# A four-way row scan and a dynamic-convolution block on one core: reciprocal deviations carried to the channels through DRAM, the norm on GpSimd

## Chip, core and metric

The kernel runs on one core of one Trainium2 chip. The metric is the device time of one launch in microseconds. Three runs of the kernel before gave 893.47 (median), 891.79 and 895.72.

## What is computed

```python
# x: (8, 64, 64, 64) float32
# 1. four scans over rows or columns, each new = cur + relu(conv9(prev)), 64 -> 64 channels
# 2. on the result x, per image (weights 5x5 per image and channel, from the pooled image):
out = depthwise_conv5x5(x, dyn_w(mean(x)))
u = out.mean(1, keepdims=True); s2 = square(out - u).mean(1, keepdims=True)
out = (out - u) * rsqrt(s2 + 1e-6)                 # over the 64 channels
out = ln2_w * out + ln2_b
out = gelu(einsum('bchw,oc->bohw', out, w_expand)) # 64 -> 256, exact gelu
gx = sqrt(sum(square(out), (2, 3)))                # per image and wide channel
nx = gx / (gx.mean(1) + 1e-6)
out = gamma * (out * nx) + beta + out
return einsum('bohw,co->bchw', out, w_shrink) + x  # 256 -> 64
```

## The kernel before

The first part, `scans` (lines 97 to 533), runs the four scans. The change leaves its loops as they are. It ends near 500 us of the profile.

The second part, `block_two` (from line 536), works on 16 units, `UNITS`: a unit is half an image, 32 lines of 64 columns, held as 128 partitions (64 channels times the parity of the line) by 1024 elements (`UCOLS`). The five engines run five programs that are written out by hand and meet at semaphores. Each program walks the same slots `s` from -1 to 20 (`SLOTS_RUN`), and in slot `s` handles several units at different stages. VectorE is in slot `s` when it adds the taps of unit `s`.

The stages of a unit `u`, with the engine and the slot:

- TensorE, slot u-1: `convolve`, five of the 5x5 taps in a split of high and low parts: 30 matmuls of 512 columns in six pieces, into PSUM banks 0 to 3 (two sets, by `u % 2`). They need `x_hi` (ScalarE, `split_high`), `x_lo` (GpSimd, `split_low`) and the diagonal weights (GpSimd, `make_dyn`, once in two units).
- ScalarE, slot u-1: five taps as products (`product`, line 764): one into `part`, four into `prod`. GpSimd adds the four in slot u (`add_product`, line 709).
- VectorE, slot u: ten taps (`take_tap`, line 883), each reading one image and the PSUM sum; the last writes `inner`. Then GpSimd adds `part` to `inner` (`add_inner`, line 722).
- Slot u+1, the statistics over channels: ScalarE squares `inner` (`square`, 772), TensorE sums both with small matmuls (`statistics`, 1075), ScalarE squares the mean (777), VectorE makes the variance (`make_var`, 891 and 893), ScalarE its root (783, after a table load), VectorE the reciprocal `rstd` of 128 x 128 (900). `rstd` holds the reciprocals on 16 of the partitions, by group of columns and line parity.
- Slot u+2: TensorE carries `rstd` to all 128 partitions with a 0/1 matrix, `spread` (`widen`, 1086, four matmuls for each half of the unit), into PSUM bank 7. VectorE multiplies `inner` by it (`norm`, 907, two halves of 512). TensorE expands (`expand`, 1100) into the one pair of banks 4 and 5, four times per unit: for each half `c` of the columns, for each half `m` of the wide channels. ScalarE takes each with `gelu` (795, with a table load per slot) and, at the end of the slot, sums the squares of both `m` (`add_squares`, 807), which wait for all four gelus. The squares are written over the same `squares` buffer that `square` uses.
- After every second unit: `sum_energy`, `root_energy`, `respond` scale the shrinking weights of the image.
- Slot u+5: TensorE `shrink` (1121, two calls), VectorE `finish` (937), SyncE `store` (684).

SyncE's queue holds, per slot, `cross(s + 2)` (lines 675 and 677: two transfers within SBUF that bring the lines of the other parity for the cross taps of unit s+2, once the taps of unit s are done), then `store(s - 5)` (two transfers to DRAM).

## Time and profile before

| what | value |
|---|---|
| median of three runs | 893.47 us |
| the profiled execution's own time | 893.85 us |
| its span, first to last instruction | 892.0 us |
| TensorE busy | 816.9 us (92%) |
| VectorE busy | 604.4 us (68%) |
| ScalarE busy | 433.2 us (49%) |
| GpSimd busy | 454.5 us (51%) |
| granted TensorE clock, mean | 0.971 |

The shares are over the whole span, of which the scans take more than half. Busy time is the time in which an engine has an instruction under way. Idle time in a table stands with the engine's next instruction and the one that released it. A duration in a row runs to the end of the instruction; the next one on the same engine may begin about 0.1 us before that end.

### The profile page before, as it was taken

Reading aid. Unit: us, or ns where it says so; the run is one execution under the profiler, and the core shown is the slowest. Engines: PE = TensorE matmul, PEld = TensorE weight load, DVE = VectorE, ACT = ScalarE, POOL = GpSimd, SP = SyncE. Lnnn points to the kernel's source line nnn. Section 1 sums busy time; section 2 is a strip of 40 time slices with the busy share of each in tenths; the row PEclk is TensorE's granted clock in tenths of the full one; section 3 lists DMA queues with packets and bytes.
Section 4 is the critical chain, followed back from the end, with each engine's and each line's share of the span. In section 5 each row is a group of like instructions: output and inputs, shape, how many; then the busy total and the mean of one; then the engine's idle time right before and its main releaser. Section 6 shows DMA issues by size and latency. Waiting matters only on the chain. (4 is left out here: it accounts for less than half of the span.)

```text
span 892.0 us, 16129 instructions
## 1 busy us (share of the span) xinstructions
PE 816.9 (92%) x5639; PEld 666.5 (75%) x5639; DVE 604.4 (68%) x1127; ACT 433.2 (49%) x520; POOL 454.5 (51%) x443
## 2 busy tenths in 40 slices
PE   5999999999999999999999675889999999999775
PEld 5999999999999999999999654455454555545231
DVE  4666666666666666678888657777887778888722
ACT  5690005777750000000000154798989898988662
POOL 2333333333323333368888466767777776765500
PEclk9999999999999999999999788889999999999997
DMA  6750000000000000000000100110222222223123
GB/s 139 170 141 0 0 0 1 0 0 0 0 1 1 0 0 0 1 1 0 0 0 0 47 0 24 34 36 24 48 47 47 47 47 47 47 47 71 24 48 71
DMA packets 51189, 26.99 MB, mean 30 GB/s; under 512 B 40720, under 2 KB 49104, under 8 KB 51152
## 3 DMA queue, kind: packets, MB, share of 16 engines
q1 hardware_dynamic: 51152, 26.51, 13.2%
q8 instruction: 22, 0.36, 0.2%
q14 instruction: 15, 0.12, 0.0%
HBM read 9.98 MB, written 8.39 MB: 21 GB/s over the span
## 5 line engine op out<-in xcount | busy, mean ns | idle before, releaser
L487 PE MATMUL psum<-line_hi,taps_hi 128*128 128x256 f32 x1270 | 203.0, 292 | 11.8 <-DVE taps_lo L383 8.6
L501 PE MATMUL psum<-line_lo,taps_hi 128*128 128x256 f32 x1270 | 202.5, 291 | 0.8 <-DVE line_lo L436 0.8
L495 PE MATMUL psum<-line_hi,taps_lo 128*128 128x256 f32 x1270 | 202.0, 291 | 0.0
L436 DVE SCALAR_TENSOR_TENSOR line_lo<-psum,rest 128x256 fp32r<-128x256 f32 x254 | 108.2, 426 | 123.6 <-POOL rest L263 115.3
L487 PEld LDWEIGHTS psum<-line_hi,taps_hi 128*128 128x128 f32 x1270 | 177.1, 192 | 13.0 <-issue 9.3
L501 PEld LDWEIGHTS psum<-line_lo,taps_hi 128*128 128x128 f32 x1270 | 176.4, 191 | 2.0 <-DVE line_lo L436 1.8
L495 PEld LDWEIGHTS psum<-line_hi,taps_lo 128*128 128x128 f32 x1270 | 176.7, 191 | 0.0
L263 POOL TENSOR_TENSOR rest<-x,line_hi 128x256 f32<-128x256 f32 x127 | 82.9, 653 | 168.5 <-DVE line_hi L427 168.5
L709 POOL TENSOR_TENSOR part<-part,prod 128x960 f32<-128x960 f32 (+2 forms) x64 | 145.2, 2269 | 24.3 <-ACT part L764 17.5
L315 ACT ACTIVATE by_h<-x (+1 forms) x128 | 85.7, 670 | 106.1 <-DVE x L416 104.5
L263 POOL TENSOR_TENSOR rest<-by_h,line_hi 128x256 f32<-128x256 f32 x127 | 91.5, 721 | 83.4 <-DVE line_hi L427 83.4
L416 DVE TENSOR_TENSOR x<-line_hi,line_lo 128x256 f32 (+1 forms) x190 | 105.5, 555 | 0.2
L883 DVE SCALAR_TENSOR_TENSOR psum<-x,tap_all,psum 128x930 f32<-128x930 f32 (+2 forms) x80 | 96.7, 1209 | 1.3
L1100 PE MATMUL psum<-normed,expand_w 64*128 64x512 f32 x256 | 75.0, 663 | 22.6 <-ACT wide L795 17.1
L764 ACT ACTIVATE prod<-x,tap_all 128x960 f32<-128x960 f32 (+2 forms) x64 | 70.1, 1101 | 37.5 <-POOL part L709 30.1
L883 DVE SCALAR_TENSOR_TENSOR psum<-crossed,tap_cross,psum 128x992 f32<-128x992 f32 (+1 forms) x64 | 80.7, 1261 | 10.3 <-PE psum L1060 9.4
L722 POOL TENSOR_TENSOR inner<-inner,part 128x1024 f32<-128x1024 f32 x16 | 37.9, 2367 | 86.5 <-DVE inner L883 86.5
L795 ACT ACTIVATE wide<-psum,expand_bias 128x1024 f32<-128x1024 f32 x64 | 70.9, 1109 | 20.9 <-PE psum L1100 20.7
L1060 PE MATMUL psum<-x_hi,dyn_hi 128*128 128x512 f32 x160 | 70.3, 439 | 9.1 <-DVE inner L883 5.8
L751 ACT ACTIVATE x_hi<-x 128x1024 fp32r<-128x1024 f32 x16 | 16.7, 1051 | 126.2 <-PEq L106 121.7
L1121 PE MATMUL psum<-wide,shrink_now 128*64 128x512 f32 x256 | 67.1, 653 | 3.7 <-DVE shrink_now L928 2.9
L427 DVE SCALAR_TENSOR_TENSOR line_hi<-psum,x 128x256 fp32r<-128x256 f32 x127 | 54.0, 425 | 21.9 <-PE psum L487 8.6
(129 smaller groups left out, 899.3 us busy)
## 6 DMA issues: line engine op xcount, KB each, us to landing
stage<-in_x_dram SPq DMA_DIRECT2D x32, 256.0 KB, 4.1
out_dram<-x SPq DMA_DIRECT2D x32, 256.0 KB, 4.4
crossed<-x SPq DMA_DIRECT2D x16, 256.0 KB, 3.5
crossed<-x SPq DMA_DIRECT2D x16, 240.0 KB, 3.6
fc_in<-in_L_conv_w_fc_dram SPq DMA_DIRECT2D x2, 100.0 KB
taps<-in_L_conv_k_td_dram SPq DMA_DIRECT2D x2, 80.0 KB, 3.3
taps<-in_L_conv_k_dt_dram SPq DMA_DIRECT2D x2, 80.0 KB, 3.3
taps<-in_L_conv_k_lr_dram SPq DMA_DIRECT2D x2, 80.0 KB, 3.5
```

Of the source, the lines that this page charges most:

```text
L263: pool.tensor_tensor(rest[:, slot % 2, :].rearrange("p (b i) -> p b i", b=B), x_line, line_hi[:, (slot + 1) % SLOTS, :, REACH:REACH + WP]. ...
L315: act.activation(dst, src, ACT.Copy).then_inc(turned, 1)
L416: dve.tensor_tensor(kept_line(s, row_of(s, k)), line_hi[:, made, :, part].bitcast(F32), line_lo[:, made, :, part].bitcast(F32), ALU.add).t ...
L436: dve.scalar_tensor_tensor(out=line_lo[:, (slot + 1) % SLOTS, :, part], in0=as_lines(line_ps[slot][:, 0:LINE]), scalar=0.0, in1=as_lines(r ...
L487: mm = pe.matmul(line_ps[slot][:, 0:LINE], taps_hi[:, s, d, :], line_hi[:, slot, :, d:d + WP], start=(d == 0), stop=(d == OFFSETS - 1))
L495: pe.matmul(line_ps[slot][:, 0:LINE], taps_lo[:, s, d, :], line_hi[:, slot, :, d:d + WP], start=False, stop=False, skip_group_check=True)
L501: mm = pe.matmul(line_ps[slot][:, 0:LINE], taps_hi[:, s, d, :], line_lo[:, slot, :, d:d + WP], start=False, stop=(d == OFFSETS - 1), skip_ ...
L709: pool.tensor_tensor(dst, dst, other, ALU.add).then_inc(part_step, 1)
L795: act.activation(wide[:, m, :, u % WIDE, c * COLS:(c + 1) * COLS], exp_ps[:, :, :], ACT.Gelu, bias=expand_bias[:, m:m + 1]).then_inc(gelu_ ...
L883: dve.scalar_tensor_tensor(out=dst, in0=src, scalar=weight, in1=here, op0=ALU.mult, op1=ALU.add).then_inc(tap_step, 1)
L1060: mm = pe.matmul(conv_ps[:, 2 * (u % 2) + c, :], weight[:, b % 2, n, :, :].rearrange("p o c -> p (o c)"), image[:, u % 2, CROWS * c:CROWS ...
L1100: mm = pe.matmul(exp_ps[:, hp, :], expand_w[half, m, :], normed[half, c, :], start=True, stop=True)
```

## The change

- `rstd` no longer goes through TensorE. SyncE stores it to a DRAM scratch of 2 x 128 x 128 (`spread_rstd`), waits until it has landed, and reads it back with two transfers, one for each line parity, each to 64 partitions (`rstd_wide`, 128 x 1024). `widen`, `spread` and its preparation in the scans go.
- `norm` moves from VectorE (two halves) to GpSimd (one multiplication of 128 x 1024), into a double buffer `normed` for whole units. In GpSimd's program it stands behind `add_inner` of the unit after it, ahead of the products.
- One tap, ("up", 3), moves from ScalarE with its addition on GpSimd to VectorE: eleven taps there, four products, three additions.
- `expand` goes by channels first: both column halves for `m` = 0, then for `m` = 1. So `add_squares` of `m` = 0 stands between the gelus and that of `m` = 1 opens the next slot; both write to a buffer of their own, `dump`. For the last two units, three pairs of PSUM banks serve in turn.
- The statistics, `make_var`, `root` and `rstd` come earlier in the slot; `inner` has two buffers in place of three; the energy of an image is summed one slot later; SyncE issues the store before the cross lines.

The diff, cut to its core:

```diff
 DVE_TAPS = [("cross", 0), ("cross", 1), ("cross", 3), ("cross", 4), ("up", 0), ("up", 4), ("down", 0), ("down", 4),
-            ("down", 3), ("cross", 2)]
+            ("down", 3), ("up", 3), ("cross", 2)]
 MIDDLE = [("down", 2), ("up", 2)]
-SIDES = [("up", 1), ("down", 1), ("up", 3)]
+SIDES = [("up", 1), ("down", 1)]
...
-        INNERS = 3
+        INNERS = 2
+        EXP_SETS = 3
+        FREE_CONV = 4 * (UNITS - 2)
...
-        normed = sb("normed", [P, 2, COLS])
+        rstd_wide = sb("rstd_wide", [P, UCOLS])
+        normed = sb("normed", [P, 2, UCOLS])
+        dump = sb("dump", [P, 2 * UCOLS], BF16)
...
+        rstd_dram = nc.dram_tensor("rstd_dram", [2, P, STAT_COLS], F32, kind="Internal").ap()
...
+        def exp_set(e):
+
+            first = 4 if e < FREE_CONV else (4, 0, 2)[(e - FREE_CONV) % EXP_SETS]
+            return psum[:, first:first + 2, :]
...
+            def spread_rstd(u):
+
+                sp.wait_ge(rstd_ready, u + 1)
+                if u > 1:
+                    sp.wait_ge(rstd_spread, 32 * (u - 1))
+                sp.dma_start(rstd_dram[u % 2], rstd[:, u % 2, :]).then_inc(rstd_stored[u % 2], 16)
+                sp.wait_ge(rstd_stored[u % 2], 16 * (u // 2 + 1))
+                if u > 0:
+                    sp.wait_ge(normed_ready, u)
+                rows = rstd_dram[u % 2].rearrange("(g q) n -> g (q n)", g=4)
+                for h in range(2):
+                    mine = rows[:, SUBS * h * STAT_COLS:SUBS * (h + 1) * STAT_COLS].rearrange("(a g) n -> a g n", a=1)
+                    sp.dma_start(rstd_wide[C * h:C * h + C, :].rearrange("p (g n) -> p g n", g=4),
+                                 mine.to_broadcast([C, 4, SUBS * STAT_COLS])).then_inc(rstd_spread, 16)
+
             cross(0)
             for s in SLOTS_RUN:
+                if s - 1 in range(UNITS):
+                    spread_rstd(s - 1)
+                if s >= 5:
+                    store(s - 5)
                 if s + 2 < UNITS:
                     cross(s + 2)
-                if s >= 5:
-                    store(s - 5)
             sp.wait_ge(stored, 32 * UNITS)
...
+            def norm(u):
+                pool.wait_ge(rstd_spread, 32 * (u + 1))
+                if u > 1:
+                    pool.wait_ge(exp_done, 4 * (u - 1))
+                image = inner[:, u % INNERS, :, :].rearrange("p j w -> p (j w)")
+                pool.tensor_tensor(normed[:, u % 2, :], image, rstd_wide[:, :], ALU.mult).then_inc(normed_ready, 1)
+
             pool.wait_ge(taps_known, 1)
             pool.wait_ge(dyn_ready, 1)
-            for u in range(UNITS):
-                for n in range(1, N_ACT):
-                    add_product(u, n)
-                if u + 2 < UNITS:
-                    split_low(u + 2)
-                if u % 2 == 0 and u // 2 + 1 < B:
-                    make_dyn(u // 2 + 1)
-                add_inner(u)
+            for s in range(UNITS + 2):
+                w, e = s - 1, s - 2
+                if w in range(UNITS):
+                    add_inner(w)
+                if e >= 0:
+                    norm(e)
+                if s < UNITS:
+                    for n in range(1, N_ACT):
+                        add_product(s, n)
+                if s + 2 < UNITS:
+                    split_low(s + 2)
+                if s % 2 == 0 and s // 2 + 1 < B:
+                    make_dyn(s // 2 + 1)
...
-            def gelu(u, c, m):
-                act.wait_ge(exp_done, 2 * (2 * u + c) + m + 1)
+            def gelu(u, m, c):
+                act.wait_ge(exp_done, 4 * u + 2 * m + c + 1)
                 if m == 0 and u >= WIDE:
                     act.wait_ge(out_done, 2 * (u - WIDE) + c + 1)
-                act.activation(wide[:, m, :, u % WIDE, c * COLS:(c + 1) * COLS], exp_ps[:, :, :],
+                act.activation(wide[:, m, :, u % WIDE, c * COLS:(c + 1) * COLS], exp_set(4 * u + 2 * m + c),
                                ACT.Gelu, bias=expand_bias[:, m:m + 1]).then_inc(gelu_done, 1)
 
             def add_squares(u, m):
                 b, h = u // 2, u % 2
-                act.wait_ge(gelu_done, 4 * (u + 1))
+                act.wait_ge(gelu_done, 4 * u + 2 * (m + 1))
                 if h == 0 and b > 0:
                     act.wait_ge(energy_summed, b)
                 if u + m > 0:
                     act.wait_ge(energy_ready, 2 * u + m)
-                if m == 0 and u + 1 < UNITS:
-                    act.wait_ge(stats_done, u + 2)
-                act.activation(squares[:, :].bitcast(BF16).rearrange("p (a n) -> p a n", a=2),
+                act.activation(dump[:, :].rearrange("p (a n) -> p a n", a=2),
                                wide[:, m, :, u % WIDE, :], ACT.Square,
                                accum_out=energy[:, m, h:h + 1]).then_inc(energy_ready, 1)
...
-                w, e, v = s - 1, s - 2, s - 5
-
-                def products(lo, hi):
-                    if s + 1 < UNITS:
-                        for n in range(lo, min(hi, N_ACT)):
-                            product(s + 1, (n + 1) % N_ACT)
-
+                w, e, n = s - 1, s - 2, s - 3
+                if n in range(UNITS):
+                    add_squares(n, 1)
                 if 2 <= s + 2 < UNITS:
                     split_high(s + 2)
-                for i in range(4):
-                    if e in range(UNITS):
-                        gelu(e, i // 2, i % 2)
-                    products(i, i + 1)
-                    if i == 1 and w in range(UNITS):
-                        square(w)
-                products(4, N_ACT)
+                if w in range(UNITS):
+                    square(w)
+                if s + 1 < UNITS:
+                    product(s + 1, 0)
                 if w in range(UNITS):
                     square_mean(w)
                     root(w)
-                if 0 < e <= UNITS and e % 2 == 0:
-                    root_energy(e // 2 - 1)
-                if e in range(UNITS):
-                    add_squares(e, 0)
-                    add_squares(e, 1)
+                if n in range(UNITS) and n % 2 == 1:
+                    root_energy(n // 2)
+                for i, between in enumerate(((1, 2), (), (3,), ())):
+                    if e in range(UNITS):
+                        gelu(e, i // 2, i % 2)
+                    if i == 1 and e in range(UNITS):
+                        add_squares(e, 0)
+                    for p in between:
+                        if s + 1 < UNITS:
+                            product(s + 1, p)
...
-                    dve.wait_ge(normed_ready, 2 * (u - INNERS + 1))
+                    dve.wait_ge(normed_ready, u - INNERS + 1)
...
-                if e in range(UNITS):
-                    norm(e, 0)
-                take(1)
+                take(2)
                 if v >= 0:
                     finish(v, 0)
                 take(2)
-                if e in range(UNITS):
-                    norm(e, 1)
-                take(2)
-                if v >= 0:
-                    finish(v, 1)
-                if 0 < e <= UNITS and e % 2 == 0:
-                    sum_energy(e // 2 - 1)
-                take(2)
+                if n in range(UNITS) and n % 2 == 1:
+                    sum_energy(n // 2)
                 if w in range(UNITS):
                     make_var(w)
                 take(1)
                 if w in range(UNITS):
                     make_rstd(w)
                 take(1)
-                if 0 < e <= UNITS and e % 2 == 0:
-                    respond(e // 2 - 1)
+                if v >= 0:
+                    finish(v, 1)
+                take(1)
+                if n in range(UNITS) and n % 2 == 1:
+                    respond(n // 2)
                 take(N_DVE)
...
+            def expand(u, m, c):
+                e = 4 * u + 2 * m + c
+                if e == 0:
+                    pe.wait_ge(weights_ready, 1)
+                if c == 0 and m == 0:
+                    pe.wait_ge(normed_ready, u + 1)
+                if e == FREE_CONV + 1:
+                    pe.wait_ge(tap_step, N_DVE * UNITS)
+                if 0 < e <= FREE_CONV:
                     pe.wait_ge(gelu_done, e)
-                else:
-                    pe.wait_ge(weights_ready, 1)
+                elif e >= FREE_CONV + EXP_SETS:
+                    pe.wait_ge(gelu_done, e - EXP_SETS + 1)
                 for hp in range(2):
                     half = slice(C * hp, C * hp + C)
-                    mm = pe.matmul(exp_ps[:, hp, :], expand_w[half, m, :], normed[half, c, :], start=True, stop=True)
+                    mm = pe.matmul(exp_set(e)[:, hp, :], expand_w[half, m, :], normed[half, u % 2, c * COLS:(c + 1) * COLS],
+                                   start=True, stop=True)
                 mm.then_inc(exp_done, 1)
...
-                at_e(widen, 0)
-                at_v(shrink, 0)
-                at_e(expand, 0, 0)
+                        shrink(v, c)
+
+                at_v(0)
                 conv(0)
-                at_e(widen, 1)
-                at_e(expand, 0, 1)
-                at_v(shrink, 1)
-                at_e(expand, 1, 0)
                 conv(1)
-                at_e(expand, 1, 1)
+                if w in range(UNITS):
+                    statistics(w)
+                at_e(0, 0)
+                at_v(1)
                 conv(2)
-                at_w(statistics)
+                at_e(0, 1)
                 conv(3)
+                if n in range(UNITS) and n % 2 == 1:
+                    respond(n // 2)
+                at_e(1, 0)
                 conv(4)
-                if 0 < e <= UNITS and e % 2 == 0:
-                    respond(e // 2 - 1)
                 conv(5)
+                at_e(1, 1)
```

GpSimd's program in block_two, in the middle of the steady run: one slot with and one without the diagonal weights. `inner<-inner,part` is `add_inner`, `part<-part,prod` is `add_product`, `x_lo` is `split_low`. Before:

```order
L722 TENSOR_TENSOR inner<-inner,part 128x1024
L709 TENSOR_TENSOR part<-part,prod 128x960
L709 TENSOR_TENSOR part<-part,prod 128x15x63
L709 TENSOR_TENSOR part<-part,prod 128x16x63
L709 TENSOR_TENSOR part<-part,prod 128x15x63
L704 TENSOR_TENSOR x_lo<-x,x_hi 128x16x64
L731 TENSOR_TENSOR dyn_hi<-ident_half,tap_hi 128x640
L731 TENSOR_TENSOR dyn_lo<-ident_half,tap_lo 128x640
```

and with the change:

```order
L744 TENSOR_TENSOR inner<-inner,part 128x1024
L762 TENSOR_TENSOR normed<-inner,rstd_wide 128x1024
L731 TENSOR_TENSOR part<-part,prod 128x960
L731 TENSOR_TENSOR part<-part,prod 128x15x63
L731 TENSOR_TENSOR part<-part,prod 128x16x63
L726 TENSOR_TENSOR x_lo<-x,x_hi 128x16x64
L753 TENSOR_TENSOR dyn_hi<-ident_half,tap_hi 128x640
L753 TENSOR_TENSOR dyn_lo<-ident_half,tap_lo 128x640
```

The multiplication stands where the fourth addition's time was, and ahead of the other three.

ScalarE's program from one table load for gelu on (`wide` is a gelu, `prod` and `part` a product, `squares<-inner` is `square`, `mean_sq` the square of the mean). Before:

```order
L795 ACT_TABLE_LOAD
L795 ACTIVATE wide<-psum,expand_bias 128x2x512
L764 ACTIVATE prod<-x,tap_all 128x960
L795 ACTIVATE wide<-psum,expand_bias 128x2x512
L764 ACTIVATE prod<-x,tap_all 128x15x63
L772 ACTIVATE squares<-inner 128x1024
L795 ACTIVATE wide<-psum,expand_bias 128x2x512
L764 ACTIVATE prod<-x,tap_all 128x16x63
L795 ACTIVATE wide<-psum,expand_bias 128x2x512
L764 ACTIVATE prod<-x,tap_all 128x15x63
L764 ACTIVATE part<-x,tap_all 128x1024
L777 ACTIVATE mean_sq<-psum 128x128
```

and with the change, from the start of a slot's statistics:

```order
L785 ACTIVATE x_hi<-x 128x16x64
L804 ACTIVATE squares<-inner 128x1024
L798 ACTIVATE part<-x,tap_all 128x1024
L809 ACTIVATE mean_sq<-psum 128x128
L815 ACT_TABLE_LOAD
L815 ACTIVATE std<-var,eps_col 128x128
L827 ACT_TABLE_LOAD
L827 ACTIVATE wide<-psum,expand_bias 128x2x512
L798 ACTIVATE prod<-x,tap_all 128x960
L798 ACTIVATE prod<-x,tap_all 128x15x63
L827 ACTIVATE wide<-psum,expand_bias 128x2x512
L837 ACTIVATE dump,energy<-wide 128x2048
```

Square, mean and root stood behind the gelus and products, and now stand ahead of them; a sum of squares stands among the gelus.

## Rows read from the trace of the kernel before

**Rows 1.** The page: the span, and busy time by engine.
```profile
span 892.0 us, 16129 instructions
PE 816.9 (92%) x5639; PEld 666.5 (75%) x5639; DVE 604.4 (68%) x1127; ACT 433.2 (49%) x520; POOL 454.5 (51%) x443
```
**Rows 2.** Busy time in stretches: length, engines, clock, DMA share, GB/s.
```profile
537.70:557.00 19.30, 12.69 (x70) 9.41 (x70) 13.53 (x15) 9.30 (x10) 13.40 (x6) 0.83 0.11 27
557.00:577.60 20.60, 17.02 (x94) 10.08 (x94) 14.88 (x17) 15.35 (x16) 15.69 (x8) 0.92 0.10 25
...
598.00:619.40 21.40, 18.59 (x104) 11.01 (x106) 15.63 (x22) 19.35 (x23) 15.71 (x8) 0.92 0.10 25
619.40:822.50 203.10, 192.95 (x1122) 105.61 (x1120) 162.84 (x202) 183.35 (x194) 141.53 (x67) 1.00 0.24 52
679.87:720.50 40.63, 38.58 (x226) 21.11 (x224) 32.56 (x41) 36.89 (x40) 29.22 (x14) 1.00 0.23 51
822.50:838.70 16.20, 11.48 (x80) 4.88 (x78) 15.88 (x19) 11.84 (x12) 11.41 (x5) 0.97 0.16 33
838.70:892.00 53.30, 37.61 (x174) 13.22 (x170) 13.66 (x29) 24.40 (x27) 2.35 (x1) 0.85 0.23 50
```
**Rows 3.** The chain that ended last, one slot from 700.80: start, us.
```profile
700.80 2.37 POOL inner L722
703.17 2.21 POOL part L709
...
705.51 2.35 POOL part L709
...
708.88 1.04 ACT squares L772
```
**Rows 4.** Groups of ScalarE, 679.87 to 720.50: count, busy, mean ns, idle before.
```profile
L807 ACT ACTIVATE squares<-wide 128x2048 bf16<-128x2048 f32 x5 | 9.5, 1903 | 0.3
L795 ACT ACTIVATE wide<-psum,expand_bias 128x1024 f32<-128x1024 f32 x8 | 8.8, 1105 | 0.5 <-PE psum L1100 0.5
L764 ACT ACTIVATE prod<-x,tap_all 128x1008 f32<-128x1008 f32 (+2 forms) x8 | 8.8, 1100 | 2.8 <-POOL part L709 2.8
L783 ACT ACT_TABLE_LOAD x2 | 2.6, 1283 | 0.0
```
**Rows 5.** Groups of GpSimd in the same stretch.
```profile
L709 POOL TENSOR_TENSOR part<-part,prod 128x945 f32<-128x945 f32 (+2 forms) x8 | 18.2, 2276 | 0.9
L722 POOL TENSOR_TENSOR inner<-inner,part 128x1024 f32<-128x1024 f32 x2 | 4.7, 2374 | 10.6 <-DVE inner L883 10.6
L704 POOL TENSOR_TENSOR x_lo<-x,x_hi 128x1024 fp32r<-128x1024 f32 x2 | 4.0, 2011 | 0.0
```
**Rows 6.** Groups of VectorE in the same stretch.
```profile
L883 DVE SCALAR_TENSOR_TENSOR psum<-x,tap_all,psum 128x930 f32<-128x930 f32 (+3 forms) x10 | 12.1, 1207 | 0.1
...
L907 DVE TENSOR_TENSOR normed<-inner,psum 128x512 f32<-128x512 f32 x5 | 3.4, 681 | 0.0
...
L891 DVE TENSOR_TENSOR var<-psum,mean_sq 128x128 f32<-128x128 f32 x2 | 0.6, 292 | 7.6 <-ACT mean_sq L777 7.6
```
**Rows 7.** A group of TensorE in the same stretch.
```profile
L1086 PE MATMUL psum<-rstd,spread 128*128 128x128 f32 x32 | 4.3, 278 | 0.0
```
**Rows 8.** DMA issues of the whole span: count, KB each, us to landing.
```profile
out_dram<-x SPq DMA_DIRECT2D x32, 256.0 KB, 4.4
crossed<-x SPq DMA_DIRECT2D x16, 256.0 KB, 3.5
...
taps<-in_L_conv_k_rl_dram SPq DMA_DIRECT2D x2, 64.0 KB, 2.4
```
**Rows 9.** SyncE's queue around one slot: start, us of the issue.
```profile
701.23 0.60 SPq L677 DMA_DIRECT2D crossed<-x  x1
```
**Rows 10.** TensorE in time: the last unit's first expansion.
```profile
858.61 1.13 PE L1100 MATMUL psum<-normed,expand_w 64*128 64x512 f32 x4
```
**Rows 11.** VectorE in time: the last unit's reciprocal.
```profile
853.01 0.95 DVE L900 RECIPROCAL rstd<-std 128x128 f32<-128x128 f32 x1 [1.10 <-ACT std L783]
```

62 lines of the change are left out of this document (15 added, 47 removed).

## The prediction

> **What bounds the kernel now.** Read first the span and the busy shares [rows 1]: 892.0 us, TensorE busy 92%, the others about half. Those are means over two parts. The change touches the second part only, so I read it in stretches [rows 2]. It has a fill (four slots, 537.70 to 619.40, 81.7 us), a steady run of ten slots from 619.40 to 822.50 (203.1 us, 20.31 a slot), the last unit's slot (16.20) and a drain (53.30). A pair of steady slots, 679.87 to 720.50, takes 40.63 us: TensorE is busy for 38.58, ScalarE for 36.89, VectorE for 32.56, GpSimd for 29.22. No engine is full, so what ends each wait must be read. The chain of waits [rows 3] runs at 700.80 through GpSimd's `add_inner` (2.37) and two of its additions (2.21, 2.35), and only then reaches ScalarE's square at 708.88. The groups say why: ScalarE idles 2.8 us a pair before its products, released by GpSimd's additions [rows 4], since a product needs its `prod` buffer emptied, and the square stands behind two such products. VectorE then waits for the squared mean, 7.6 us a pair [rows 6]. So the bound is a ring: last tap, `add_inner`, two additions, products, square, statistics, variance, last taps.
>
> **The change, part by part**, for one pair of slots. Instructions that follow at once on ScalarE, VectorE or GpSimd start about 0.1 us before the earlier one's end, so I count 1.00 us for a product of 1.10 and 0.60 for a norm of 0.68.
>
> 1. *The square goes ahead of the products.* Square, mean and root of a unit come before the slot's gelus. From the last tap on: `add_inner` 2.4, square 1.0, statistics 1.1, mean 0.3, with some 0.3 of handovers: 5.1 us, where VectorE has four taps and a finish to do (about 5.8). Most of its 7.6 us of waiting [rows 6] goes. What is late next is ScalarE itself.
> 2. *ScalarE*: 36.89 busy [rows 2], less two products of 1.00, is 34.9. The 2.8 us before products [rows 4] goes: the first product is now needed after square, root and two table loads (1.28 each), some 10 us into the slot, when GpSimd has added the first two. New idle time: 0.3 a slot for the statistics; 0.1 before each of two sums of squares, which need the gelu just ahead finished; and 0.6 before the fourth gelu. This last comes so: after the second gelu TensorE has an expansion (1.1), two pieces of convolution (2.4) and the next expansion (1.1), 4.7 us with handovers, against ScalarE's sum of squares, gelu and product, 3.9 to 4.1. So 1.1 a slot at most; part of the old idle of the other groups [rows 4] is the same handovers. I take 1.7 a pair: **36.6 us a pair**, 18.3 a slot.
> 3. *VectorE*: 32.56, less four norms of 0.60 [rows 6], plus two taps of some 1.16 (the group's mean is 1.21 to the end): 32.5. A slot of its own work without waits is then about 16.1, which lets a short slot follow a long one; the pair stays at 36.6.
> 4. *TensorE*: the 32 records of `widen` go, 4.3 us [rows 7], 4.1 without overlap: 34.5 of 36.6. The respond of a pair keeps its wait for ScalarE.
> 5. *GpSimd*: two additions of 2.28 go, two multiplications of 128 x 1024 come. No row shows this one. Bounds: 2.01 (the subtraction of the same size) and 2.37 (`add_inner`) [rows 5]; I take 2.37, same inputs and output type. Busy 29.4 of 36.6. It stands ahead of the three additions, so they end near 11.8 us into a slot, about when the third buffered product is asked for (13 us or later): covered. If that cover were gone each late microsecond would count once a slot. On VectorE the two halves cost 1.36, on GpSimd 2.37 [rows 5, 6]. The Trainium skill (GPSIMD Engine Reference, Engine selection) says to give elementwise work on two inputs to VectorE, GpSimd being about twice as slow. By it, with the extra 1.0 us on the path, 16 units would give back 16 us. The row with GpSimd's 10.6 us of waiting a pair [rows 5] speaks for hidden.
> 6. *The trip through DRAM.* No row shows it. It is two transfers in sequence: the store of 64 KB, and two reads of 256 KB. Landing is 2.4 us after the issue for the nearest small one, 4.4 at most; 3.5 to 4.4 for 256 KB [rows 8]. An issue takes 0.6 [rows 9]. So 0.1 + (2.4 to 4.4) + 0.6 + (3.5 to 4.4) = 6.6 to 9.5; I take 8, nearest to the crossed rows, since the pieces read are 1 KB. The cover: `rstd` is ready about 9 to 10 us into its slot, and the norm stands behind `add_inner` of the next, so 9.6 us in the short slots, 13 in the long ones. Hidden in the steady run, just. The Trainium skill (DMA: Bandwidth & Descriptors, Rules for kernel authors) says that two transfers to disjoint halves of the partitions serialize. By it the second read lands a whole transfer, up to 3.5 us, later, a trip of 11.5 and a cover that fails in short slots. The crossed pairs are such halves, issued 0.6 apart, and land in 3.5 and 3.6: the trace disagrees.
> 7. *SyncE's queue.* The store of the image halves waits now behind the `rstd` transfers, and the cross lines behind both. The cross lines of unit s+2 are asked for at the end of slot s as before and needed a slot later: nothing.
> 8. *Expansion by channels, two `inner` buffers, `dump`*: `inner` is free once norm of unit s-2 is done, 5 us into slot s, needed at its end: nothing. `dump` removes a wait of under 0.1.
>
> **The sum.** Steady run: five pairs, 5 x (40.6 - 36.6) = 20 us saved. Fill: the first slots have no expansions, and only VectorE's own work bounds them: 15.1, 15.1 plus about 1 for a slower clock, then 18.5 and 21.8 as ScalarE fills; 71.5 against 81.7 in [rows 2], 10.2 saved. Unit 0's eleventh tap: 1.2 lost. The last unit's slot was VectorE's own work already (15.88 busy of 16.20): nothing. Drain: the last reciprocal now ends at 853.96, 15.3 us after the last tap [rows 11], since the square stands behind four gelus; with item 1 it takes 5.1 + 1.3 (table load) + 0.3 + 0.9 = 7.6, so 7.7 saved. From there to the expansion at 858.61 [rows 10] it is 4.65 now, and 8 + 2.4 + 0.2 = 10.6 with the trip: 6.0 lost. Three pairs of banks save about 1.0, one sum of squares (1.9) [rows 4] moves ahead of the end: 2.9 saved. TensorE idles some 5 us in the trip and is slow after it, as in the drain now (clock 0.85 [rows 2]): 3 lost. Together 1.6 saved, in bounds of 3 either way. Sum: 20 + 10.2 - 1.2 + 1.6 = 30.6 us saved. The profiled execution took 893.85 (span 892.0 and 1.9 around it), 0.4 over the median 893.47, so it gives 863.3 and, by the median, 862.9: I take **863 us**.
>
> **The rivals.**
> - *ScalarE finds no waits* (the 1.7 a pair goes into handovers already counted): a pair of 34.9. For it: its old idle outside the products is only 1.0 a pair. Against it: TensorE would be 99% busy. 7 x 1.7 = 12 less: 851. Chance 0.10.
> - *TensorE's clock falls in the steady run.* It was granted 1.00 with 2.05 us of pauses in 40.63, and 0.92 with 3.6 in 20.60 [rows 2], that is, parts of each fill slot at 1.2 instead of 2.4 GHz. After the change there are 2.1 us of pauses in 36.6, each under 1.2. If it fell, an expansion and five or six convolution matmuls would run at double time, 1 to 2 us a slot: 863 + 11 x 1.5 = 880. Pauses say no, but one long wait would start it. Chance 0.10.
> - *Slower: the trip through DRAM becomes the ring.* Store, read back, norm (2.4), expansion, the four gelus with products and sums of squares, then the next square, mean, root and reciprocal: 22 to 24 us beside the trip, over two slots. It decides from a trip of about 13 us and is slower than today's pair from about 17 to 19. If 64 partitions reading the same 4 KB are slow, a trip of 20 gives a pair of 43: 863 + 7.5 x 6.4 = 911. The rows [rows 8] bound it at 9.5. Chance 0.04.
> - *It does not do what it says*: the order of the programs shows the norm, the square and the scratch transfers in place, so the one way left is that some new wait holds the ring near 20.3 a slot, with the fill's saving given back in the drain: about 892. Chance 0.03.
>
> **How the numbers follow.** My own case holds 0.73, with its unknowns (fill 4, drain 3, waits 0.8 a pair either way, trip) 855 to 873. The range is stretched upwards to the clock rival's middle, and down to 854: 854 to 880 leaves out most of the first rival, half of the second and the last two. A measurement of this kernel can tell about 0.5%, 4.5 us. Faster takes my case and the first two rivals, 0.93; within 0.5% 0.03; slower 0.04.
>
> **What would show it.** A pair of steady slots near 36.6 us, long and short in turn, ScalarE busy about 95%; VectorE's wait for the squared mean down from 7.6 to about 2 a pair; ScalarE's wait for GpSimd before products gone; clock 1.00; the 64 KB store landing in 2.4 to 4.4 us and the norm released by `add_inner` or the queue, not by the transfer; the norm at 2.4 us. I am wrong if the norm waits for the transfer in the steady run, if the granted clock there is under 1.00, or if the pair is under 35 or over 39.

## The result, and the profile after

The changed kernel takes **868.75 us** (median of 4 runs, 868.32 to 870.50) against 893.37 us (median of 4, 891.79 to 895.72): ratio 0.9726, 95% interval [0.9709, 0.9742], 24.6 us less. The forecast was 863 in 854 to 880, and faster. The sign and the mechanism held; the size came out 6 us short of the forecast, and the steady run carries most of it. One execution of experiment 10 took 1449.09 us; it ran in a slower state and is left out of that experiment's median.

The profiled execution took 868.42 us with this span and these busy shares, beside [rows 1]:

```profile
span 866.5 us, 15588 instructions
PE 782.7 (90%) x5383; PEld 635.1 (73%) x5383; DVE 610.1 (70%) x1111; ACT 413.7 (48%) x501; POOL 455.5 (53%) x443
```

TensorE lost 34 us of work and the span fell by 25.5: the one does not give the other. The stretches say where the time went. The view is busy time by stretch, with the columns of [rows 2]: length; busy time (and instructions) of TensorE, its weight loads, VectorE, ScalarE, GpSimd; clock; DMA share; GB/s. Every boundary is the end of a unit's last tap: four slots of fill, the ten steady slots, one pair of them, the last unit's slot, the drain.

```profile
538.15:554.06 15.91, 10.40 (x62) 7.64 (x62) 14.80 (x15) 6.84 (x8) 11.12 (x5) 0.82 0.31 70
554.06:570.46 16.40, 14.36 (x74) 8.63 (x74) 14.80 (x15) 11.71 (x13) 15.82 (x8) 0.84 0.32 67
570.46:589.25 18.79, 14.17 (x77) 7.86 (x77) 14.92 (x15) 16.81 (x19) 13.39 (x6) 0.91 0.24 61
589.25:611.27 22.02, 18.37 (x98) 9.61 (x96) 15.96 (x22) 19.77 (x23) 15.82 (x8) 0.92 0.19 51
611.27:799.22 187.95, 173.40 (x964) 86.18 (x960) 168.47 (x192) 174.09 (x185) 142.17 (x67) 1.00 0.37 87
687.15:725.08 37.93, 34.70 (x192) 17.23 (x192) 33.90 (x39) 35.04 (x38) 29.30 (x14) 1.00 0.36 86
799.22:815.29 16.07, 8.33 (x62) 2.70 (x60) 15.82 (x17) 11.68 (x13) 11.39 (x5) 1.00 0.25 62
815.29:866.50 51.21, 35.04 (x152) 10.79 (x148) 11.10 (x25) 25.00 (x27) 7.01 (x3) 0.80 0.30 66
```

Against [rows 2], stretch by stretch: the steady run saved 203.10 - 187.95 = 15.2 us (forecast 20), the fill 81.7 - 73.1 = 8.6 (forecast 10.2), the last slot 0.1, the drain 53.30 - 51.21 = 2.1 (forecast 1.6), and the last tap of unit 0 came at 538.15 instead of 537.70, 0.4 later (forecast 1.2). The pair fell from 40.63 to 37.93 us where 36.6 was forecast: **1.3 us a pair are missing**. That holds for the first four pairs. The fifth, in whose long slot GpSimd has no diagonal weights to make, takes 36.19, so the five together miss 4.9 us.

The pair now has a slot of 16.06 and one of 21.87 us in turn. The waits the change was aimed at are gone, as the groups of the pair show (line, engine, operation, names, shape, count | busy, mean ns | idle before, by releaser). ScalarE, beside [rows 4]:

```profile
L827 ACT ACTIVATE wide<-psum,expand_bias 128x1024 f32<-128x1024 f32 x8 | 8.8, 1106 | 1.7 <-PE psum L1108 1.6
L798 ACT ACTIVATE prod<-x,tap_all 128x960 f32<-128x960 f32 (+2 forms) x6 | 6.4, 1094 | 0.0
L804 ACT ACTIVATE squares<-inner 128x1024 f32<-128x1024 f32 x2 | 2.1, 1044 | 0.7 <-POOL inner L744 0.7
```

GpSimd, beside [rows 5], with the new multiplication:

```profile
L744 POOL TENSOR_TENSOR inner<-inner,part 128x1024 f32<-128x1024 f32 x2 | 4.8, 2383 | 8.1 <-DVE inner L911 8.1
L762 POOL TENSOR_TENSOR normed<-inner,rstd_wide 128x1024 f32<-128x1024 f32 x2 | 4.8, 2380 | 0.0
```

VectorE, beside [rows 6]:

```profile
L941 DVE SCALAR_TENSOR_TENSOR resp<-resp,gamma 128x2 f32<-128x2 f32 x1 | 1.2, 1191 | 0.0
L919 DVE TENSOR_TENSOR var<-psum,mean_sq 128x128 f32<-128x128 f32 x2 | 0.6, 288 | 1.4 <-ACT mean_sq L809 1.4
```

The products' wait for GpSimd went from 2.8 to 0, VectorE's wait for the squared mean from 7.6 to 1.4, and the norm costs 2.38 us without a wait. But one row is new in kind: **`resp<-resp,gamma`, two elements on each partition, takes 1.19 us.** Before, the same instruction took 220 to 222 ns in all eight images. VectorE in time, about 15 us into a long slot (start us, us; in brackets the idle time before and what ended it):

```profile
680.01 0.16 DVE L937 TENSOR_SCALAR resp<-psum 128x1 f32<-128x1 f32 x1 [1.65 <-PE psum L1117]
680.20 0.16 DVE L939 RECIPROCAL resp<-resp 128x1 f32<-128x1 f32 x1
680.40 1.19 DVE L941 SCALAR_TENSOR_TENSOR resp<-resp,gamma 128x2 f32<-128x2 f32 x1
681.62 0.17 DVE L944 TENSOR_SCALAR resp<-resp 128x2 f32<-128x2 f32 x1
681.83 0.29 DVE L947 TENSOR_TENSOR shrink_now<-shrink_t,resp 128x128 f32<-128x128 f32 x1
```

and GpSimd at the same time:

```profile
680.31 1.26 POOL L753 TENSOR_TENSOR dyn_lo<-ident_half,tap_lo 128x640 fp32r<-128x640 f32 x1
```

VectorE's step begins 0.09 us after GpSimd's `dyn_lo` multiplication and ends at 681.59, 0.02 after it. It happens at 642.62, 680.40, 718.32 and 756.25 (1.03 to 1.21 us). In the other four images of the changed kernel, and in all eight before the change, GpSimd stands idle at that moment or has just ended, and the step takes 0.22. A busy row hid a wait: no view of waits lists this one.

The trip through DRAM, in SyncE's queue (start, us of the issue):

```profile
695.31 0.33 SPq L696 DMA_DIRECT2D rstd_dram<-rstd  x1
696.86 1.28 SPq L703 DMA_DIRECT2D rstd_wide<-rstd_dram  x2
698.18 1.35 SPq L689 DMA_DIRECT2D out_dram<-x  x2
```

and the page's list of DMA issues (count, KB each, us to landing), beside [rows 8]:

```profile
rstd_wide<-rstd_dram SPq DMA_DIRECT2D x32, 256.0 KB, 5.4
out_dram<-x SPq DMA_DIRECT2D x32, 256.0 KB, 5.4
...
rstd_dram<-rstd SPq DMA_DIRECT2D x16, 64.0 KB, 1.5
```

The reciprocal is ready at 695.2, the last read lands near 702.9 (an estimate: second issue at about 697.5, plus the median 5.4): 7.7 us. The norm starts at 705.69, behind `add_inner`, so the trip has some 2.8 us to spare in the slot where it has least. Over all units the norm waited for the transfer once, 11.0 us in the drain.

### The profile page after: what moved, and what is told of

Same layout as the page of the kernel before. It is cut to its first block and busy times, and to the rows that moved or that the text cites. A ratio compares the mean times of both kernels' runs of the same rounds, so it can differ in the third digit from the quotient of the medians.

```text
span 866.5 us, 15588 instructions
## 1 busy us (share of the span) xinstructions
PE 782.7 (90%) x5383; PEld 635.1 (73%) x5383; DVE 610.1 (70%) x1111; ACT 413.7 (48%) x501; POOL 455.5 (53%) x443
## 5 line engine op out<-in xcount | busy, mean ns | idle before, releaser
L731 POOL TENSOR_TENSOR part<-part,prod 128x960 f32<-128x960 f32 (+2 forms) x48 | 108.6, 2263 | 20.4 <-ACT prod L798 15.8
L911 DVE SCALAR_TENSOR_TENSOR psum<-x,tap_all,psum 128x930 f32<-128x930 f32 (+3 forms) x96 | 116.5, 1213 | 1.7
L1074 PE MATMUL psum<-x_lo,dyn_hi 128*128 128x512 f32 x160 | 67.6, 423 | 0.0
```

The lines of the kernel that those rows point to most:

```text
L731: pool.tensor_tensor(dst, dst, other, ALU.add).then_inc(part_step, 1)
L911: dve.scalar_tensor_tensor(out=dst, in0=src, scalar=weight, in1=here, op0=ALU.mult, op1=ALU.add).then_inc(tap_step, 1)
L1074: mm = pe.matmul(conv_ps[:, 2 * (u % 2) + c, :], weight[:, b % 2, n, :, :].rearrange("p o c -> p (o c)"), image[:, u % 2, CROWS * c:CROWS ...
```

## The experiments

Two questions: what are the missing 1.3 us of a pair, and what is each part of the change worth? In all edits below the lines marked - are the changed kernel's. In experiments 1, 2 and 5 two constants are copied to free columns of a PSUM bank once, before the slots; 8 and 9 write the same data to DRAM more often. The diffs show the core of each edit.

**1. The response's constants in PSUM.**

```diff
+            act.activation(gamma_ps, kept["gamma"][:, :], ACT.Copy)
+            act.activation(shrink_ps, kept["shrink_t"][:, :, :], ACT.Copy).then_inc(fixed_ready, 1)
...
-                                         in1=kept["gamma"][:, :], op0=ALU.mult, op1=ALU.mult).then_inc(resp_step, 1)
+                                         in1=gamma_ps, op0=ALU.mult, op1=ALU.mult).then_inc(resp_step, 1)
...
-                dve.tensor_tensor(shrink_now[:, :, :], kept["shrink_t"][:, :, :],
+                dve.tensor_tensor(shrink_now[:, :, :], shrink_ps,
```

> gamma and the shrinking weights are copied once into free columns of PSUM bank 7, and the two VectorE instructions of respond that read two operands in SBUF read one of them in PSUM. Theory (VectorE instructions with two SBUF inputs wait while GpSimd runs one of its own): the multiplication by gamma falls from 1.03 to 1.21 us back to 0.22 in all images, the pair of steady slots from 37.94 to about 37.0, the time from 868.7 by four stalls of 0.97 to about 865. Rival (the step is long for another reason, or its length is hidden by the wait for TensorE): the multiplication stays near 1.1 us or the pair stays at 37.9, time 868 to 869.

Measured: 869.81 us (868.78 to 871.38), ratio 0.9737 [0.9723, 0.9750]. No gain, a miss of the theory. The trace shows why; VectorE in time:

```profile
680.42 0.22 DVE L948 SCALAR_TENSOR_TENSOR resp<-resp,psum 128x2 f32<-128x2 f32 x1
680.67 0.88 DVE L951 TENSOR_SCALAR resp<-resp 128x2 f32<-128x2 f32 x1
```

The product with gamma is back at 0.22 us in every image. The next step, "+1" on two elements, now ends (681.55) with GpSimd's `dyn_lo`, which runs from 680.27 for 1.26 us in this kernel. The stall moved by one instruction. The "+1" takes 0.56 to 0.90 us in four images, each time until `dyn_lo` ends. So a step with two inputs in SBUF is held, one with one in SBUF and one in PSUM is not, and a `tensor_scalar` from SBUF to SBUF is held as well. The reciprocal of one column (680.22, SBUF to SBUF) ran in 0.16 us while `dyn_hi` was at work: that form is not held.

**2. No step of the response that can be held.** The product with gamma is written to PSUM too, and "+1" reads it there.

```diff
+        more_ps = stat_ps[:, 2 * STAT_COLS + 4:2 * STAT_COLS + 4 + HALVES]
...
-                dve.scalar_tensor_tensor(out=resp[:, 4, :], in0=resp[:, 1, :], scalar=resp[:, 3, 0:1],
-                                         in1=kept["gamma"][:, :], op0=ALU.mult, op1=ALU.mult).then_inc(resp_step, 1)
+                dve.scalar_tensor_tensor(out=more_ps, in0=gamma_ps, scalar=resp[:, 3, 0:1],
+                                         in1=resp[:, 1, :], op0=ALU.mult, op1=ALU.mult).then_inc(resp_step, 1)
...
-                dve.tensor_scalar(resp[:, 5, :], resp[:, 4, :], 1.0, None, ALU.add).then_inc(resp_step, 1)
+                dve.tensor_scalar(resp[:, 5, :], more_ps, 1.0, None, ALU.add).then_inc(resp_step, 1)
```

> One step further than the run that moved gamma and shrink_t to PSUM: the product with gamma is now written to PSUM too, so that the '+1' reads PSUM, and none of the five small VectorE steps of the response has more than one full-size operand in SBUF and none goes from SBUF to SBUF except the reciprocal of one column. Theory (VectorE's small steps from SBUF to SBUF wait for the pair of ports that GpSimd holds during its 1.26 us multiplication for the dynamic weights): the +1 takes about 0.1 to 0.2 us instead of 0.88 in every image, four long slots get 0.9 to 1.0 shorter (21.87 to about 20.9, pair 36.9 to 37.1), total 868.75 - 4 x 0.97 = 864.9 (864 to 866.5). Rival (the small step waits whatever its operands are, so the stall goes on to the last step, the product with shrink_t): that step takes 0.9 us or more instead of 0.2 to 0.3 and the total stays at 868 to 870.

Measured: 866.28 us (865.66 to 868.70), ratio 0.9707 [0.9693, 0.9721]. The ten steady slots take 184.99 us instead of 187.95, the first four long ones 20.96 to 21.27. Both steps are short in all eight images (count, then ns min/median/max):

```profile
L949 DVE SCALAR_TENSOR_TENSOR psum<-psum,resp x8: 227/227/229, 607.1 to 849.7; 128x2 f32<-128x2 f32 x8
```

```profile
L952 DVE TENSOR_SCALAR resp<-psum x8: 159/159/160, 607.3 to 849.9; 128x2 f32<-128x2 f32 x8
```

Here `dyn_lo` ran from 681.28 for 1.27 us, right across the product at 681.41, the "+1" at 681.68 and the product with `shrink_t` at 681.87 (0.29 us). The same overlap, no stall.

**3. GpSimd's work moved instead.** Operands stay in SBUF; the dynamic weights are multiplied out one slot earlier.

```diff
-                if s % 2 == 0 and s // 2 + 1 < B:
-                    make_dyn(s // 2 + 1)
+                if s == 0:
+                    make_dyn(1)
+                if s % 2 == 1 and s // 2 + 2 < B:
+                    make_dyn(s // 2 + 2)
```

> The response as in the changed kernel, with its operands in SBUF; only GpSimd's work for the dynamic weights of an image (five small multiplications, the last one 1.26 us) is done one slot earlier, in the slot that has no response. If the collision of the two engines is the cause, resp x gamma takes 0.22 us in every image again, the long slots lose about 0.97 each and the total is 864 to 866.5, as without the SBUF operands. Rival (it is not GpSimd but a late event of ScalarE or TensorE that ends the 1.19 us): the product still takes 1.0 to 1.2 us and the total stays at 868 to 870. A third outcome: the moved multiplications delay GpSimd's own chain in the short slot (norm, additions), which shows as a wait of the last tap or of the square and costs up to 1.3 per pair: 869 to 879.

(The work is two multiplications of 1.26 us, not five as that text says.) Measured: 867.06 us (865.62 to 867.72), ratio 0.9710 [0.9697, 0.9723], just above the 864 to 866.5 expected; steady run 184.92 us, pair 37.13. The step, with its operands where they were:

```profile
L943 DVE SCALAR_TENSOR_TENSOR resp<-resp,gamma x8: 221/221/222, 605.7 to 847.4; 128x2 f32<-128x2 f32 x8
```

Two remedies that share nothing, one on each engine, give the same 184.9 us. That settles the stall: **while GpSimd runs an elementwise instruction from SBUF that began first, a VectorE step with two SBUF inputs, or a `tensor_scalar` from SBUF to SBUF, stands until it ends.** The Trainium skill (SBUF — State Buffer, Who interferes with whom) states this as an exclusive lock held for a whole instruction, taken by a VectorE instruction with two SBUF inputs or in a two-port mode, and not by one with at most one SBUF input outside those modes. The traces agree, with 1.19 against 0.22 us and 0.88 against 0.16. No trace names the mode in which the `tensor_scalar` ran.

In whole executions the remedies give 1.7 to 2.5 us, less than the 3.0 of the steady run, and the ratios' intervals overlap with the changed kernel's ([0.9709, 0.9742]): that the stall costs time is read from the steady slots, not from the medians. In experiment 2 the last slot, for one, grew from 16.07 to 17.35.

**4. The tap moved back.** Ten taps on VectorE, five products on ScalarE, four additions on GpSimd, as before the change; the sum of squares writes into `squares` again for want of SBUF.

```diff
-            ("down", 3), ("up", 3), ("cross", 2)]
+            ("down", 3), ("cross", 2)]
...
-SIDES = [("up", 1), ("down", 1)]
+SIDES = [("up", 1), ("down", 1), ("up", 3)]
...
-        dump = sb("dump", [P, 2 * UCOLS], BF16)
...
-                for i, between in enumerate(((1, 2), (), (3,), ())):
+                for i, between in enumerate(((1, 2), (), (3, 4), ())):
```

> The tap ('up', 3) goes back from VectorE to ScalarE and GpSimd (ten taps, five products, four additions), all else as in the changed kernel, but the second buffer for the squares' output is shared again for want of SBUF. VectorE loses 16 x 1.22 us, ScalarE gains 16 x 1.10, GpSimd 16 x 2.3. Theory (in the changed kernel the bound is split between ScalarE, 35.0 of the pair of 37.9, and the ring through VectorE's response): the ScalarE sum becomes 35.0 + 2.2 = 37.2 of 37.9, the pair stays at 37.2 to 38.2, total 866 to 872: the moved tap was worth little. Rival (VectorE is what bounds, 33.9 + its stall): the pair falls by up to 1.0, total 858 to 864. Second rival (ScalarE bounds): pair 39.2 or more, total 879 to 888.

Measured: 870.20 us (868.09 to 871.03), ratio 0.9738 [0.9725, 0.9752], pair 38.80: its interval and the changed kernel's overlap. But the pair is above the 37.2 to 38.2 expected, and the trace shows the lock at its clearest. GpSimd has more to add and reaches its split and both multiplications just when the response comes:

```profile
679.41 2.00 POOL L725 TENSOR_TENSOR x_lo<-x,x_hi 128x1024 fp32r<-128x1024 f32 x1
681.37 1.26 POOL L752 TENSOR_TENSOR dyn_hi<-ident_half,tap_hi 128x640 fp32r<-128x640 f32 x1
682.59 1.26 POOL L752 TENSOR_TENSOR dyn_lo<-ident_half,tap_lo 128x640 fp32r<-128x640 f32 x1
```

and VectorE:

```profile
680.24 1.19 DVE L944 SCALAR_TENSOR_TENSOR resp<-resp,gamma 128x2 f32<-128x2 f32 x1
681.46 1.19 DVE L947 TENSOR_SCALAR resp<-resp 128x2 f32<-128x2 f32 x1
682.69 1.31 DVE L950 TENSOR_TENSOR shrink_now<-shrink_t,resp 128x128 f32<-128x128 f32 x1
```

Each ends with one of GpSimd's instructions (681.43 with 681.41, 682.65 with 682.63, 684.00 with 683.85), which then starts its next before VectorE's next step is there. Three steps that together take 0.68 us when nothing holds them take 3.69. The first is held by the split, a subtraction, the others by the multiplications.

**5. The tap back, and no step that can be held** (edits of 2 and 4 together).

> The kernel with the tap ('up', 3) back on ScalarE and GpSimd (870.2 us, pair 38.79), and the response's operands in PSUM as in the 866.3 us kernel. With the tap back, three small steps of the response fell on GpSimd's split, dyn_hi and dyn_lo multiplications and took 1.19, 1.19 and 1.31 us where they take 0.22, 0.17 and 0.29 alone: 3.0 us per pair. Theory: the stall goes, but ScalarE's work (35.0 + 2 x 1.1 = 37.2) sets the pair then: 37.2 to 37.6, so 5 x 1.3 = 6 less, total 863 to 866, no slower than eleven taps with the same remedy: the tap itself is worth nothing on the whole, it only changes what collides. Rival 1 (the 3.0 come off in full): pair 35.8, total 855 to 858. Rival 2 (another wait takes its place at once): total 868 to 871.

Measured: **864.14 us** (863.68 to 866.39), ratio 0.9681 [0.9662, 0.9699], the lowest time of all kernels here. The first theory's numbers hold: pair 37.24, bound by ScalarE. The pair's row, and all of ScalarE's waits in it (total us, times, longest):

```profile
683.01:720.25 37.24, 34.56 (x194) 17.25 (x193) 30.63 (x37) 36.67 (x40) 33.82 (x16) 1.00 0.35 88
```

```profile
ACT mean_sq L815 <- PE psum L1100: 0.3, 2, 0.2
```

So the eleventh VectorE tap is worth nothing that these runs show. With the stall in both, the kernels stand at 868.75 and 870.20; with it in neither, at 866.28 and 864.14, and the ratios' intervals overlap narrowly ([0.9693, 0.9721] and [0.9662, 0.9699]). The tap takes ScalarE's work out of the pair and leaves ScalarE waiting instead.

**6. The trip and GpSimd's norm undone**, the new order kept: the reciprocals go back through TensorE, and VectorE norms in two halves of 128x512.

```diff
-                if s - 1 in range(UNITS):
-                    spread_rstd(s - 1)
...
+                if e in range(UNITS):
+                    widen(e, 0)
                 at_v(0)
                 conv(0)
+                if e in range(UNITS):
+                    widen(e, 1)
                 conv(1)
...
-                take(2)
+                take(1)
+                if s - 2 in range(UNITS):
+                    norm(s - 2, 0)
+                take(1)
...
```

> The trip through DRAM and the norm on GpSimd are undone, the new order is kept: TensorE carries rstd to the channels again with eight small matmuls a slot, VectorE multiplies in two halves out of PSUM. Theory (most of the gain is the square, mean and root ahead of the gelus, and the DRAM trip with GpSimd's norm buys about 1 us a slot by taking 2.1 us from TensorE and 1.2 from VectorE): a pair of about 38.5 to 39, time 873 to 879. Rival (the way through DRAM carries the gain): 888 or more.

Measured: 879.69 us (877.24 to 881.25), ratio 0.9836 [0.9815, 0.9857], just above the 873 to 879 expected. The pair:

```profile
696.44:736.06 39.62, 38.44 (x226) 21.00 (x224) 35.18 (x43) 34.91 (x38) 24.61 (x12) 1.00 0.23 53
```

TensorE is busy for 97% of it. So the other parts (order, tap, buffers) give about 14 of the 24.6 us, and the trip with GpSimd's norm the other 11. The response is not held in this kernel. Without the trip TensorE is nearly the bound of the pair, and that fits a gain from taking 4.1 us of work off it.

**7. The order undone**, the trip kept: square, mean and root behind the gelus as before, with the matching order on VectorE and TensorE (not shown).

```diff
-                if w in range(UNITS):
-                    square(w)
-                if s + 1 < UNITS:
-                    product(s + 1, 0)
-                if w in range(UNITS):
-                    square_mean(w)
-                    root(w)
...
-                for i, between in enumerate(((1, 2), (), (3,), ())):
+                for i, between in enumerate(((1,), (2,), (3,), (0,))):
...
+                    if i == 1 and w in range(UNITS):
+                        square(w)
+                if w in range(UNITS):
+                    square_mean(w)
+                    root(w)
...
```

> The DRAM trip and GpSimd's norm stay, but square, mean and root go back behind the gelus and products, on ScalarE, TensorE and VectorE. Theory (the trip is hidden only because the reciprocals are ready in the first half of the slot): the norm then waits for the transfer in every slot, a slot takes 26 to 28 us, the time is 990 to 1020, far over the kernel before. Rival (the trip has slack either way and the order is worth what the sum said, 2 us a slot): 890 to 905.

Measured: 1041.77 us (two runs, 1036.58 and 1046.95), ratio 1.1659 [1.1603, 1.1715]: beyond even what the theory gave. The norm waits for the transfer in every unit (releaser, total us, times), and two of the longest waits are:

```profile
  DMA rstd_wide<-rstd_dram: 66.5, 16
```

```profile
ACT wide L827 <- PE psum L1106: 175.9, 47, 12.3
...
DVE var L917 <- ACT mean_sq L809: 120.9, 16, 14.8
```

TensorE's granted clock was 0.83 in the stretch from 620 to 860, where it was busy 165.98 of 240 us; in the changed kernel it is 1.00, so part of the longer time is the clock's. The trip with the old order is the slowest kernel here. The trip needs the new order; the order, as experiment 6 shows, does not need the trip.

**8. and 9. A longer trip.** The store is repeated k times before the reads, k = 2 and k = 6.

```diff
+                for again in range(2):
+                    sp.wait_ge(rstd_stored[u % 2], 16 * ((1 + 2) * (u // 2) + again + 1))
+                    sp.dma_start(rstd_dram[u % 2], rstd[:, u % 2, :]).then_inc(rstd_stored[u % 2], 16)
...
```

> Each store of the reciprocal deviations to DRAM is done three times, one after the other, before the two reads: 2 x 1.55 us (from a store's issue to the reads' issue) longer, so the trip is 7.7 + 3.1 = 10.8 us. In the profile of the changed kernel the norm starts 2.8 us after the landing in the slot where it is nearest. If the trip has a slack of 2.8 and becomes part of a ring behind it, a pair pays at most 0.3 to 0.6, and the fill and the drain 3.1: total 868.75 + 3.1 + 5 x 0.5 = 874 (872 to 876), and GpSimd waits for the transfer in every second slot. Rival 1 (the trip is on the path already, each us of it counts in each slot): 15 x 3.1 = 46 more, 900 to 915. Rival 2 (hidden everywhere, GpSimd's own order decides, the drain alone pays): 871 to 872.

Measured: 876.16 us (875.22 to 877.12), ratio 0.9809 [0.9794, 0.9824]: 3.05 us of trip cost 7.4 over the whole kernel. Reads are issued 4.60 us after the first store instead of 1.55 (first store, then reads):

```profile
698.43 0.33 SPq L696 DMA_DIRECT2D rstd_dram<-rstd  x1
...
703.03 1.28 SPq L706 DMA_DIRECT2D rstd_wide<-rstd_dram  x2
```

The norm's waits for the transfer over the kernel:

```profile
  DMA rstd_wide<-rstd_dram: 20.8, 10
```

Some 14 of the 20.8 us are the drain's (11.0 and 3.05); the other nine waits are 0.8 each. By spans: last tap of the last unit 5.0 later (815.29 to 820.30), drain 51.2 to 54.8. The steady run took 2.0 more, as expected (1.5 to 3), the fill 1.7 and the drain 3.6, where 3.1 was expected for both. But the 2.0 do not come by the ring that was expected. In the four long slots with diagonal weights the response starts where it did (14.72 to 14.75 us into the slot; 14.72 to 14.89 in the changed kernel) and ends 0.2 to 1.1 us later. The late norm has moved GpSimd's multiplications, and they now hold the "+1" for 1.2 us. So the steady slots pay through the lock, and no other cost of the longer trip is seen in them.

> The store done seven times instead of once: 6 x 1.53 us longer (measured with two more: reads issued 4.60 us after the store instead of 1.55), trip 7.7 + 9.2 = 16.9 us. This is the rival of the prediction in which the trip becomes a ring (from about 13 us on, slower than before from 17 to 19). Worked out from the slots: from the statistics of a unit to its expansion lie about 4 us of mean, root and reciprocal, the trip and 2.4 of norm, 23.3 in all, against a slot of 16.1 or 21.9 plus about 0.5. So the short slot would stretch by 6.7 and the long one by 1: pair 45 to 46, total 868.75 + 5 x 7.7 + fill and drain 15 = 920 (905 to 935). Rival (only GpSimd's own ring counts, add, trip, norm, three sums, two slots long: 8 + 17 + 2.4 + 9.1 = 36.5 per pair, under 37.9): only drain and fill pay, 882 to 892.

Measured: 927.21 us (926.33 to 928.88), ratio 1.0381 [1.0360, 1.0403]. The pair:

```profile
712.83:757.15 44.32, 36.25 (x192) 17.65 (x192) 34.76 (x39) 35.21 (x38) 29.24 (x14) 0.96 0.37 93
```

The pair pays 6.4 of the 9.2 us, all of it in the long slot (28.1 to 28.4 in the first four, 29.2 in the fifth; the short one stays 16.06), where the theory had stretched the short one. Here the response itself starts over 5 us later (20.17 to 20.42): the ring was real and its total well placed. From 8 and 9: in the steady slots the trip has 2.3 us of slack by the waits of experiment 8 (3.05 - 0.8), or 2.8 by the estimate above; in the drain every microsecond of it counts; at 16.9 us the kernel is slower than before, 927 against 893. A straight line between the two runs, an estimate from two points, goes through 893 at a trip near 13 us, lower than the 17 to 19 of the prediction.

**10. GpSimd's norm moved to VectorE**, whole (128x1024, both inputs in SBUF), trip kept.

```diff
+            def norm(u):
+                dve.wait_ge(rstd_spread, 32 * (u + 1))
+                dve.wait_ge(inner_ready, u + 1)
+                if u > 1:
+                    dve.wait_ge(exp_done, 4 * (u - 1))
+                image = inner[:, u % INNERS, :, :].rearrange("p j w -> p (j w)")
+                dve.tensor_tensor(normed[:, u % 2, :], image, rstd_wide[:, :], ALU.mult).then_inc(normed_ready, 1)
...
```

> The trip through DRAM stays, but the multiplication of 128 x 1024 is VectorE's, behind its second tap, both inputs in SBUF. If nothing contends it takes 1.1 to 1.3 us, GpSimd loses 2.4 us a slot, and the time is 868 to 872. If VectorE and GpSimd exclude each other where VectorE reads two SBUF inputs, the multiplication's record is lengthened by what is left of GpSimd's instruction at that moment, up to 2.3 us more, and the time is 875 to 895.

Measured: 868.95 us (868.67 to 870.17, three executions), ratio 0.9723 [0.9706, 0.9741]: the same as on GpSimd. But two things changed. VectorE's busy time grew to 35.10 us in the pair, and without the norm GpSimd ends `dyn_lo` 1.3 us earlier in its slot, so the response is not held in any image (0.22). The pair is 37.84 us, 0.1 below the changed kernel, but 0.7 above the 37.13 of the kernels without the stall. By that comparison the norm on VectorE costs about 0.7 a pair, and the stall that it happens to avoid hides the cost. VectorE takes 1.22 us (median 1225 ns) for what GpSimd does in 2.38. The lock shows on the other side: VectorE's norm starts at 690.39, GpSimd's additions right behind it, and

```profile
690.50 8.06 POOL L731 TENSOR_TENSOR part<-part,prod 128x960 f32<-128x960 f32 x3
```

the three additions take 8.06, where the same three take 7.07 in the changed kernel. GpSimd waits 10.7 us a pair for the last tap anyway, so nothing comes of it. Twice in the fill the norm itself is held, behind an addition of GpSimd's that began at 574.28 and ended at 576.53:

```profile
574.51 3.10 DVE L927 TENSOR_TENSOR normed<-inner,rstd_wide 128x1024 f32<-128x1024 f32 x1
```

**11. The expansion by rows first.**

```diff
-                        gelu(e, i // 2, i % 2)
-                    if i == 1 and e in range(UNITS):
+                        gelu(e, i % 2, i // 2)
+                    if i == 2 and e in range(UNITS):
...
```

> Undoes the expansion by channels first alone: order (rows 0, channels 0), (rows 0, channels 1), (rows 1, channels 0), (rows 1, channels 1), so the first energy sum of ScalarE can start only after the third Gelu and fills no gap after the second. Theory (ScalarE then waits for TensorE's third expansion where it now sums the energy): up to 0.6 to 1.0 us per pair and a later response, total 871 to 876. Rival (the order of the four expansions is worth nothing, ScalarE is not continuous in this stretch anyway): 868 to 870.

Measured: 870.78 us (870.70 to 871.08), ratio 0.9747 [0.9729, 0.9765], 2.0 over the changed kernel and at the edge of what was expected, with intervals that overlap. The steady run hardly differs (188.75), and the pair is 37.95. That looks as if the theory's 0.6 to 1.0 a pair were not there, but the trace shows the stall covering it. ScalarE's waits for the expansions grew from 1.6 to 2.5 us a pair, and the response starts 0.6 to 0.8 us later in the slot. It ends where it did, since `dyn_lo` ends at the same place (684.71 here) and now holds the product for 0.23 us only:

```profile
684.27 0.45 DVE L941 SCALAR_TENSOR_TENSOR resp<-resp,gamma 128x2 f32<-128x2 f32 x1
```

Against the 37.13 of the kernels without the stall this pair is 0.8 longer. So the order of the expansions is worth nothing beside the stall and probably 0.6 to 0.8 us a pair without it; no run has the rows first and no stall. In the fill it gives 2.2 us (75.3 against 73.1), in the drain the rows first are 1.7 quicker.

**12. A try at a faster kernel**: experiment 3, the response two taps later, and the last expansion ahead of the last piece of convolution.

```diff
-                take(1)
+                take(3)
                 if n in range(UNITS) and n % 2 == 1:
                     respond(n // 2)
...
                 conv(4)
+                at_e(1, 1)
                 conv(5)
-                at_e(1, 1)
```

> Three moves of order on the changed kernel, nothing computed otherwise: GpSimd's multiplications for the dynamic weights one slot earlier (that alone gave 867.06, pair 37.14), VectorE's steps of the response two taps later, and the last expansion of a unit ahead of the last piece of the convolution. VectorE stood 1.65 us per pair waiting for TensorE's mean of the energy; with two more taps (2 x 1.2 us) ahead of it that wait is covered. Theory (with the collision gone the pair is set by this wait, and behind it by ScalarE's 35.0 us of work plus its waits for GpSimd and TensorE of 1 to 1.5): pair 36.0 to 36.3, total 867 - 5 x 0.9 = 862.5 (861 to 865). Rival (TensorE waits for the later response before its last product, and passes it on): pair stays at 37.1 or longer, total 866 to 869.

Measured: 866.39 us (864.99 to 867.37), ratio 0.9695 [0.9677, 0.9713], no different from 867.06, and the pair is still 37.14. VectorE's wait for the response (1.65) is gone, but it now waits 3.3 us a pair for TensorE's convolution, and the slots are 17.66 and 19.48 with the same sum. All of ScalarE's waits in the pair:

```profile
ACT mean_sq L811 <- PE psum L1091: 1.5, 2, 0.8
ACT wide L829 <- PE psum L1110: 0.7, 3, 0.3
```

34.92 us of work and 2.2 of waits are the 37.14. In this kernel VectorE has time to spare. The reading that fits experiments 2, 3 and 12 is that the pair is ScalarE's work plus its waits for TensorE. It is not ScalarE's work alone: experiment 5 has 1.7 us more of it and 0.3 of waits, for nearly the same pair (37.24). No run shortens the stretch on TensorE between two gelus by itself, so this reading is argued, not shown.

Not tried: a single buffer more or fewer for `inner`, the `dump` buffer by itself, and experiments 10 and 11 on a kernel without the stall.

## Why the prediction was right, and where it was off

*Item 1, the square ahead of the products*: right. The wait for the squared mean fell to 1.4 (about 2 forecast), and experiment 6 puts 14 us on the order and what goes with it.

*Item 2, ScalarE 34.9 and 1.7 of idle, pair 36.6*: the bound that was named fits experiments 2, 3, 5 and 12. Work came to 35.04 (34.91 in experiment 3). The idle time is 2.2 where nothing collides (1.7 for expansions, 0.3 for statistics, 0.2 small), and the pair then 37.13. So 0.5 of the miss of 1.3 is this term. The itemised sum of the prediction gave 1.1 a slot "at most", which is the 2.2 measured; the step that went wrong is the discount to 1.7. The wait sits where the prediction had it, before the fourth gelu, with 0.79 and 0.86 us in experiment 3 for the 0.6 forecast. The third gelu does not wait.

*Item 3, VectorE 32.5, 16.1 for a slot of its own*: the short slot is 16.06. The pair's busy time is 33.90, and 32.99 where nothing collides. **This is the step that failed**: "the pair stays at 36.6" had the response at its length in the trace of before, 0.22 us a step, and no account of what GpSimd does beside it: the hold was a term put at nothing, without a reason. The change put the response right behind GpSimd's split, and the lock added 0.97 us to VectorE in the long slot. Through the last tap and GpSimd's `add_inner` it reached ScalarE, whose square waits 0.7 for `add_inner` in the pair and not at all in experiment 3. It costs 0.8 in each of four pairs and nothing in the fifth, 3.0 us of the steady run (187.95 to 184.92). With the 0.5 above that is the 1.3 of a pair, and 3.0 + 1.9 is the 4.9 of the steady run. VectorE's own work was also put 0.5 too low, which cost nothing while it waits.

*Item 4, TensorE 34.5*: 34.70.

*Item 5, the norm 2.37 and hidden*: 2.38, no wait in the steady run. By the rule of the Trainium skill weighed there (GPSIMD Engine Reference, Engine selection) 16 us would have been given back; it held for the duration (experiment 10: 1.22 against 2.38) and not for the path: the norm on VectorE gives nothing back, and costs some 0.7 a pair once the stall is out of the comparison.

*Item 6, the trip 8 us, in 6.6 to 9.5*: 7.7, but by two errors that cancel, so the close match is luck. The store landed in 1.5 us (bounds 2.4 to 4.4), the reads in 5.4 (bounds 3.5 to 4.4). The nearest rows were a 64 KB load and crossed pairs; a store of the same size was quicker, and a read in which 64 partitions fetch the same 4 KB slower. The Trainium skill (DMA: Bandwidth & Descriptors, Rules for kernel authors) says that transfers to disjoint halves serialize, and the prediction took this for a second read that lands a whole landing time later, a trip of 11.5. That did not happen: both reads of a pair are issued within 1.3 us, the median of all 32 is 5.4 and the longest 6.4, and the norm, which starts 10.5 us after the reciprocal in the short slots (705.69 against 695.2), waited nowhere outside the drain. The page gives no such time, though; whether the two reads take turns on the same engines, no run here shows, and the crossed pairs' 3.5 and 3.6 us, issued 0.6 apart, do not decide it. The reciprocal came 8.1 us into the short slot (687.15 to 695.28) where 9 to 10 were forecast, so the slack, put at "hidden, just", is 2.3 to 2.8 us.

*Items 7 and 8, SyncE's queue and the buffers at nothing*: no row speaks against it, and no run tests it. The output stores land in 5.4 us instead of 4.4, and nobody waits for them.

*Fill 71.5*: 73.1. The first two slots took 15.9 and 16.4 against 15.1 and 16.1, with VectorE's 14.80 of work in each. VectorE waits in them for the squared mean, 0.8 and 1.3 us, which the forecast had not put in.

*Drain*: from last tap to reciprocal 8.0 us (815.29 to 823.31; 7.6 forecast), from there to the first expansion at 833.52 10.2 (10.6 forecast), and it began at a low clock after 4.94 us of waiting: 2.08 us for what takes 1.13 (clock 0.80 over the drain). The sum came to 2.1 for 1.6. These two terms hold; those of 1.0, 1.9 and 3 us have no run of their own.

*The rivals*: the clock stayed at 1.00. That the trip becomes a ring was right in kind and happened in experiment 9, at 927 us for 16.9; its thresholds were too high, 17 to 19 us against some 13. The prediction put 22 to 24 us beside the trip into two slots; in experiment 9 it is 44.32 - 16.9 = 27.4, and fill and drain pay as well. "ScalarE finds no waits" did not occur, but experiment 5 shows what it looks like: 0.3 us of waits in 37.24.

## What to carry to other kernels

When a change shifts one engine's work in time, look at what GpSimd and VectorE do side by side at the new place, the small instructions too: a step on two elements can cost 1.2 us, it counts as busy time, and no list of waits shows it. The cure is an operand in PSUM or a shift of the other engine's work. Look also whether such a stall is in the kernel that you compare with: in experiments 10 and 11 it came or went with the edit and hid what the edit itself costs. And an operation taken off an engine is worth nothing until you know which engine's work plus waits make up the period. Here the best reading is ScalarE with TensorE; experiment 12, which took one wait away from VectorE, left the pair at 37.14 and only moved the wait.

## What the runs showed of the hardware

- GpSimd's elementwise instruction from SBUF holds up VectorE instructions with two SBUF inputs that begin after it (128x2: 1.19 instead of 0.22 us; 128x128: 1.31 instead of 0.29; 128x1024: 3.10 instead of 1.22) and a `tensor_scalar` from SBUF to SBUF (0.56 to 1.20 instead of 0.17). With an input in PSUM, and for a reciprocal of one column from SBUF, no hold was seen. A VectorE norm with two SBUF inputs that began first held GpSimd's addition for 1.0 us in the same way.
- A 64 KB store to DRAM landed in 1.5 us from its issue, and an issue of reads could follow 1.55 us behind it; two reads of 256 KB, in each of which 64 partitions fetch the same 4 KB in four pieces, landed in 5.4. Transfers of 256 KB within SBUF took 3.6 in the same kernel, and the reads of `x` from DRAM, 256 KB each, 4.0.
- The same multiplication of 128x1024 in fp32 took 2.38 us on GpSimd and 1.22 on VectorE.
- TensorE's granted clock was 1.00 while it was busy 34.70 of 37.93 us, 0.96 at 36.25 of 44.32 (experiment 9), and 0.83 at 166 of 240 (experiment 7). These are three stretches and no rule.
